# Two score banks for each exponential in an attention over 1920 keys

## The chip, the cores and the metric

The kernel runs on one core of one Trainium2 chip. The metric is the device time of one execution in microseconds (us); the median of several runs counts. Engines: PE is TensorE, ACT is ScalarE, DVE is VectorE, POOL is GpSimd, SP issues DMAs. PEld is PE's loading of weights, which runs beside its matmuls.

## The reference

A block of eight layers on x (16 batches, 256 tokens, 256 channels), each added to x. The change touches the fifth, an attention in which batches aren't kept apart: all 4096 tokens attend to the 16 x 120 = 1920 context tokens of all batches.

```python
# 8 heads, DIM_HEAD 128, SCALE = 128 ** -0.5
qh = _split_heads(jnp.einsum('bnq,qi->bni', x, Wq))
kh = _split_heads(jnp.einsum('bmc,ci->bmi', context, Wk))
vh = _split_heads(jnp.einsum('bmc,ci->bmi', context, Wv))
sim = jnp.einsum('hid,hjd->hij', qh, kh) * SCALE
mean = jnp.mean(sim, axis=-1, keepdims=True)
sim = (sim - mean) * ATTN_MATRIX_SCALE + mean
attn = jax.nn.softmax(sim, axis=-1)
out = jnp.einsum('hij,hjd->hid', attn, vh)
out = out.transpose(1, 2, 0, 3) ...
return jnp.einsum('bniv,iq->bnq', out, Wout) + bout
```

The mean falls out of the softmax, so the kernel takes exp(1.5 x SCALE x score - bias), with the row's maximum in the bias.

## The kernel before

The stage is `global_attention_stage`. The work goes by head (8), in a head by quad (8 quads of 512 tokens), in a quad by row tile j (4 of 128 tokens). The heads but the first and last run in a loop of the device. All products are exact to float32 by three passes of PE on a high and a low part of each operand (`three_passes`, L1811 to L1813): ACT writes the high part (`high`, L1739), DVE the rest (`low`, L1647).

While the probabilities of quad n are multiplied with the values, the scores and exponentials of quad n+1 are made, row tile by row tile. The orders are written by hand in a function `head` of each engine:

- PE, for row tile j: `scores` of j, one PSUM bank of 480 keys for each c (banks 0 to 3, 12 matmuls), then j's share of the 15 key tiles (4, 4, 4 and 3). A k-step waits for the low part of key tile k, turns key tile k+2 (`turn`, L1853: four transposes of a 128x128 block into bank 4 or 5) and makes the three passes on k. Between stand, for j=0, turns 0 and 1 and half of the output projection; for j=1 the other half (`output`, L1864); for j=2 `queries` of a later quad (L1834). `values` of a key share (L1828) stand in quad 0 of a head (before turn 8) and three times in the quad that turns the head.
- DVE: `maximum` (four maxima L1653, one over them, and the bias L1656), then `low_probs` of the key tiles turned in j.
- ACT: `high_probs` of the turned key tiles (two ahead for j=0, one for j=1 to 3) and between them the four exponentials of j, `exponential` (L1760), each out of one bank, with its sum in `part_sum`. In j=3 only key tile 14 is left to be turned, and the four follow one another.

The prob_t buffers are three deep, the banks for turns two. A bank of scores is free for PE when its exponential has raised `exped`. DVE's `sums` adds up `part_sum` once a quad. Before the first head, the first quad's scores, exponentials and values are made without other work beside them.

Of the kernel before, what the change touches and what calls it, by code (L numbers as in the profile page):

```python
# [22 lines left out]
ACT = mybir.ActivationFunctionType  # L23
AX = mybir.AxisListType

P = 128
# [1427 lines left out]
def global_attention_stage(nc, w, ctx):  # L1454
# [7 lines left out]
    chunk = 4 * NCTX  # L1462
    chunks = B // 4
    KEYS = B * NCTX
    KT = KEYS // P
    QT = 4
# [10 lines left out]
    def sb(name, shape, dt=F32):  # L1477
        return ctx.enter_context(nc.sbuf_tensor(f"global_{name}", shape, dt))
# [14 lines left out]
    q_high, q_low = sb("q_high", [P, 2, QW], F32R), sb("q_low", [P, 2, QW], F32R)  # L1493
    spare = w.held["spare"]
    prob = [spare[:, 0:QT * KEYS].rearrange("p (j c) -> p j c", j=QT), sb("prob", [P, QT, KEYS])]
    part_sum = sb("part_sum", [P, 2, QT, chunks])
    inverse = sb("inverse", [P, 2, QT])

    top = sb("top", [P, chunks])
# [13 lines left out]
    scores_psum, bias_ready, exped = sig("scores_psum"), sig("shifted"), sig("exped")  # L1513
# [18 lines left out]
    with nc.Block() as block:  # L1532
        @block.sync
        def _(sp):
            sp.dma_start(bout[:, :], io["L2_xattn_bout"].partition_broadcast(P)).then_inc(bout_loaded.sem, 16)
            sp.dma_start(ctx_t[:, :, :], io["ctx_t"].rearrange("(k p) b j -> p k (b j)", p=CP)
                         ).then_inc(loaded.sem, 16)
# [62 lines left out]
    def over_heads(eng, head):  # L1600

        head(0, True, False)
        with eng.Fori(1, heads - 1) as h:
            head(h, False, False)
        head(heads - 1, False, True)

    with nc.Block() as block:
# [126 lines left out]
        @block.scalar  # L1734
        def _(act):
            def high(dst, psum, is_there, n, ready):

                act.wait_ge(is_there.sem, is_there.count(n))
                act.activation(dst, psum, ACT.Copy).then_inc(ready.sem, 1)  # L1739

            def high_queries(n, par):
                high(q_high[:, par, :], w.psum[:, 7, :], q_psum, n, q_high_ready)

            def high_keys(h, c):
                high(k_high[:, c * chunk:(c + 1) * chunk], w.psum[:, c, 0:chunk], k_psum, h * chunks + c,
                     k_high_ready)

            def high_values(h, s, bank):
                tiles = slice(shares[s][0], shares[s][-1] + 1)
                high(v_high[:, tiles, :], w.psum[:, bank, 0:len(shares[s]) * dim]  # L1750
                     .rearrange("p (k d) -> p k d", d=dim), v_psum, h * QT + s, v_high_ready)

            def high_probs(n, k):
                high(prob_t_high[:, k % RING, :], w.psum[:, 4 + k % 2, :], prob_t_psum, n * KT + k, high_ready)

            def exponential(n, par, j, c):

                if c == 0:
                    act.wait_ge(bias_ready.sem, bias_ready.count(n * QT + j))
                act.activation(prob[par][:, j, c * chunk:(c + 1) * chunk], w.psum[:, c, 0:chunk], ACT.Exp,  # L1760
                               bias=bias[:, j % 2:j % 2 + 1], scale=scale,
                               accum_out=part_sum[:, par, j, c:c + 1]).then_inc(exped.sem, 1)

            def head(h, first, last):
                for t in range(QUADS):
                    n = h * QUADS + t
                    after = not (last and t == LAST)
                    turns_head = t == LAST and after
                    for j in range(QT):
                        ahead = list(turned_in[j])  # L1770
                        if j == 2 and not (last and t >= LAST - 1):
                            high_queries(n + 2, t % 2)
                        if turns_head and j == 0:
                            for c in range(chunks):
                                high_keys(h + 1, c)
                            lead = 5
                        else:
                            lead = 2 if j == 0 else 1
                        for k in ahead[:lead]:
                            high_probs(n, k)  # L1780
                        for c in range(chunks):
                            if after:
                                exponential(n + 1, (t + 1) % 2, j, c)
                            if t == 0 and j == 1 and c == 1:
                                high_values(h, 3, 7)
                            if turns_head and (j, c) in ((1, 1), (2, 1), (3, 0)):
                                high_values(h + 1, j - 1, 7)
                            for k in ahead[lead + c:lead + c + 1]:
                                high_probs(n, k)
                    act.wait_ge(attn_psum.sem, attn_psum.count(n))  # L1790
                    act.activation(attn_t[:, :], w.psum[:, 6, :], ACT.Copy).then_inc(attn_ready.sem, 1)

            for c in range(chunks):
                high_keys(0, c)
            high_queries(0, 0)
            for j in range(QT):
                for c in range(chunks):
                    exponential(0, 0, j, c)
                if j < 3:
                    high_values(0, j, 4 + j % 2)  # L1800
                if j == 2:
                    high_queries(1, 1)
            over_heads(act, head)

        @block.tensor
# [962 lines left out]
def chosen_attention_stage(nc, w, ctx):  # L2768
# [454 lines left out]
    ("last of all", experts_stage),  # L3223
    ("hold long", place_powers),
    ("compute", global_attention_stage),
    ("hold long", place_selective),
    ("compute", ternary_and_spectrum_stage),
# [88 lines left out]
```

## Time and profile before

| | |
|---|---|
| median of 3 runs | 4632.93 us (4632.79 to 4633.71) |
| the profiled execution | 4636.67 us |
| its span | 4634.9 us |
| PE busy | 4151.4 us |
| DVE busy | 3322.0 us |
| ACT busy | 2232.4 us |
| PE's mean granted clock | 0.946 |

The profile is of one execution. "Busy" counts the time in which at least one instruction of an engine runs; a matmul's duration includes its way through the array, so that PE's starts say more than its durations. "Idle before" is the time an engine stood still ahead of an instruction, and what released it. A granted clock of 1.00 is 2.4 GHz.

### The profile page before, as it was taken

What the parts mean: (1) busy time and instruction counts of PE and PEld (TensorE: products, weight loads), DVE (VectorE), ACT (ScalarE), POOL (GpSimd) and SP (SyncE); (2) the same over time, 40 slices, a digit from 0 to 9 for tenths busy, and PEclk for the clock granted to TensorE, in tenths of its full rate; (3) what the DMA queues carried; (4) which work ended last, traced back from release to release, by engine and by line L of the source; (5) the groups of instructions that cost most, each with busy time, mean ns of one, the idle gap of its engine ahead of it and who ended that gap; (6) DMA issues with size and microseconds to landing.
All of it is one profiled execution on the core that took longest, in us unless ns stands there. A gap on an engine that the chain in (4) does not pass through costs nothing. (4 is left out here: it accounts for less than half of the span.)

```text
span 4634.9 us, 72082 instructions
## 1 busy us (share of the span) xinstructions
PE 4151.4 (90%) x23376; PEld 3267.9 (71%) x23376; DVE 3322.0 (72%) x7934; ACT 2232.4 (48%) x5314; POOL 529.9 (11%) x982
## 2 busy tenths in 40 slices
PE   7998988999699999999999999999985888888686
PEld 6876766777387877778777777777863665656555
DVE  6985667666677777777777677777767888876455
ACT  3545655555365565655555555565531232322332
POOL 1331010111500000000000000001142111111300
PEclk9998999999799999999999999999975999989699
DMA  3000000000000000000000000000020000000101
GB/s 93 0 0 37 0 1 0 0 0 0 18 3 2 4 2 4 1 2 4 2 4 2 4 1 2 4 2 2 1 72 1 1 1 0 0 1 0 40 0 36
DMA packets 33797, 40.58 MB, mean 9 GB/s; under 512 B 5550, under 2 KB 30006, under 8 KB 33466
## 3 DMA queue, kind: packets, MB, share of 16 engines
q1 hardware_dynamic: 32732, 37.03, 2.7%
q8 instruction: 128, 2.10, 0.2%
q14 instruction: 137, 1.12, 0.1%
q10 hardware_dynamic: 800, 0.33, 0.0%
HBM read 32.90 MB, written 4.19 MB: 8 GB/s over the span
## 5 line engine op out<-in xcount | busy, mean ns | idle before, releaser
L1739 ACT ACTIVATE global_prob_t_high<-psum 128x512 fp32r<-128x512 f32 x960 | 570.7, 601 | 588.9 <-PE psum L1853 588.9
L1647 DVE TENSOR_TENSOR global_prob_t_low<-psum,global_prob_t_high 128x512 fp32r<-128x512 f32 x960 | 657.2, 690 | 251.0 <-ACT global_prob_t_high L1739 237.0
L1653 DVE TENSOR_REDUCE global_top<-psum 128x1 f32<-128x480 f32 x1024 | 666.9, 658 | 110.8 <-PE psum L1813 106.3
L1811 PE MATMUL psum<-global_prob_t_high,global_v_low 128*128 128x512 f32 x960 | 455.6, 475 | 1.0
L1811 PE MATMUL psum<-global_k_high,global_q_low 128*128 128x480 f32 x1024 | 390.6, 381 | 17.4 <-ACT spare L1760 14.8
L1813 PE MATMUL psum<-global_k_high,global_q_high 128*128 128x480 f32 x1024 | 391.1, 382 | 0.0
L1812 PE MATMUL psum<-global_k_low,global_q_high 128*128 128x480 f32 x1024 | 388.9, 380 | 0.0
L1812 PE MATMUL psum<-global_prob_t_low,global_v_high 128*128 128x512 f32 x960 | 379.7, 396 | 0.0
L1813 PE MATMUL psum<-global_prob_t_high,global_v_high 128*128 128x512 f32 x960 | 379.6, 395 | 0.0
L1760 ACT ACTIVATE spare<-psum,global_bias 128x480 f32<-128x480 f32 x512 | 337.8, 664 | 16.5 <-DVE global_bias L1656 15.1
L1760 ACT ACTIVATE global_prob<-psum,global_bias 128x480 f32<-128x480 f32 x512 | 337.9, 663 | 1.2
L1382 ACT ACTIVATE moe_gated<-psum,moe_weight 128x256 f32<-128x256 f32 x512 | 215.2, 472 | 228.3 <-PE psum L1436 212.9
L1853 PEld LDWEIGHTS psum<-ident,global_prob 128*128 128x128 f32 x1920 | 233.4, 141 | 99.3 <-DVE global_prob_t_low L1647 35.8
L1853 PEld LDWEIGHTS psum<-ident,spare 128*128 128x128 f32 x1920 | 234.0, 141 | 96.1 <-DVE global_prob_t_low L1647 33.6
L1853 PE MATMUL psum<-ident,global_prob 128*128 128x128 f32 x1920 | 284.1, 273 | 18.9 <-DVE global_prob_t_low L1647 17.9
L1853 PE MATMUL psum<-ident,spare 128*128 128x128 f32 x1920 | 284.2, 273 | 17.8 <-DVE global_prob_t_low L1647 17.8
L1811 PEld LDWEIGHTS psum<-global_k_high,global_q_low 128*128 128x128 f32 x1024 | 193.5, 189 | 59.9 <-ACT spare L1760 15.6
L390 POOL COPY powers<-ones 128x128 f32<-128x128 f32 x1 | 0.4, 414 | 1979.8 <-PE psum L1834 1979.8
L1812 PEld LDWEIGHTS psum<-global_k_low,global_q_high 128*128 128x128 f32 x1024 | 193.0, 189 | 33.5
L1813 PEld LDWEIGHTS psum<-global_k_high,global_q_high 128*128 128x128 f32 x1024 | 193.5, 189 | 29.7
L1813 PEld LDWEIGHTS psum<-global_prob_t_high,global_v_high 128*128 128x128 f32 x960 | 180.6, 188 | 42.3
L1434 PE MATMUL psum<-moe_we_high,moe_xn_low 128*128 128x512 f32 x512 | 204.1, 399 | 0.0
(455 smaller groups left out, 8593.3 us busy)
## 6 DMA issues: line engine op xcount, KB each, us to landing
x_res<-in_x SPq DMA_DIRECT2D x8, 512.0 KB, 9.8
moe_we<-in_expert_t SPq DMA_DIRECT2D x8, 512.0 KB, 7.6
out<-x_res SPq DMA_DIRECT2D x4, 1024.0 KB, 8.5
cho_wqkv<-in_L_ffn_Wqkv SPq DMA_DIRECT2D x2, 1536.0 KB
self_ctx_t<-in_ctx_t SPq DMA_DIRECT2D x2, 1440.0 KB, 13.6
sel_w<-in_L_xattn_W SPq DMA_DIRECT2D x2, 1024.0 KB, 11.2
global_ctx_t<-in_ctx_t SPq DMA_DIRECT2D x1, 1440.0 KB
sel_ctx_t<-in_ctx_t SPq DMA_DIRECT2D x1, 1440.0 KB
```

What stands on the lines that cost most here:

```text
L390: pool.tensor_copy(re[:, :, 0], w.ones[:, :])
L1382: last = act.activation(gated[:, local % RING, h, :], w.lane(s)[:, 1 + p % 3, h * D:(h + 1) * D], ACT.Relu, scale=weight[:, s, x:x + 1])
L1434: pe.matmul(bank, xn_low[:, s, k, :], we_high[pair], start=False, stop=False)
L1647: dve.tensor_tensor(dst, psum, high.bitcast(F32), ALU.subtract).then_inc(ready.sem, 1)
L1653: ins = dve.tensor_reduce(top[:, c:c + 1], w.psum[:, c, 0:chunk], AX.X, ALU.max)
L1739: act.activation(dst, psum, ACT.Copy).then_inc(ready.sem, 1)
L1760: act.activation(prob[par][:, j, c * chunk:(c + 1) * chunk], w.psum[:, c, 0:chunk], ACT.Exp, bias=bias[:, j % 2:j % 2 + 1], scale=scale, a ...
L1811: pe.matmul(to, lhs_low, rhs_high, start=start, stop=False)
L1812: pe.matmul(to, lhs_high, rhs_low, start=False, stop=False)
L1813: return pe.matmul(to, lhs_high, rhs_high, start=False, stop=stop)
L1853: last = pe.transpose(w.psum[:, 4 + k % 2, j * P:(j + 1) * P], prob[par][:, j, k * P:(k + 1) * P], w.ident[:, :])
```

## The change

An exponential reads two banks at once, 128 x 2 x 480 elements, and writes the 960 probabilities beside each other. `part_sum` holds two sums a row tile in place of four. The instruction raises `exped` by 2, so that all counts that other engines wait for stay as they were; a wait for bank 0 or 1 is now met when both have been read. The highs keep their places in the loop over c, where the calls for odd c fall out.

```diff
-    part_sum = sb("part_sum", [P, 2, QT, chunks])
+    part_sum = sb("part_sum", [P, 2, QT, chunks // 2])
...
-                act.activation(prob[par][:, j, c * chunk:(c + 1) * chunk], w.psum[:, c, 0:chunk], ACT.Exp,
+                act.activation(prob[par][:, j, c * chunk:(c + 2) * chunk].rearrange("p (c x) -> p c x", x=chunk),
+                               w.psum[:, c:c + 2, 0:chunk], ACT.Exp,
                                bias=bias[:, j % 2:j % 2 + 1], scale=scale,
-                               accum_out=part_sum[:, par, j, c:c + 1]).then_inc(exped.sem, 1)
+                               accum_out=part_sum[:, par, j, c // 2:c // 2 + 1]).then_inc(exped.sem, 2)
...
                         for c in range(chunks):
-                            if after:
+                            if after and c % 2 == 0:
                                 exponential(n + 1, (t + 1) % 2, j, c)
...
             for j in range(QT):
-                for c in range(chunks):
+                for c in range(0, chunks, 2):
                     exponential(0, 0, j, c)
```

ACT, a steady quad, row tile j=2 from the high part of the queries on, and j=3, before (`global_prob_t_high` is `high_probs`):

```order
L1739 ACTIVATE global_q_high<-psum 128x512
L1739 ACTIVATE global_prob_t_high<-psum 128x512
L1760 ACTIVATE spare,global_part_sum<-psum,global_bias 128x480
L1739 ACTIVATE global_prob_t_high<-psum 128x512
L1760 ACTIVATE spare,global_part_sum<-psum,global_bias 128x480
L1739 ACTIVATE global_prob_t_high<-psum 128x512
L1760 ACTIVATE spare,global_part_sum<-psum,global_bias 128x480
L1739 ACTIVATE global_prob_t_high<-psum 128x512
L1760 ACTIVATE spare,global_part_sum<-psum,global_bias 128x480
L1739 ACTIVATE global_prob_t_high<-psum 128x512
L1760 ACTIVATE spare,global_part_sum<-psum,global_bias 128x480 x4
L1791 ACTIVATE global_attn_t<-psum 128x512
```

The same place with the change:

```order
L1739 ACTIVATE global_q_high<-psum 128x512
L1739 ACTIVATE global_prob_t_high<-psum 128x512
L1760 ACTIVATE spare,global_part_sum<-psum,global_bias 128x960
L1739 ACTIVATE global_prob_t_high<-psum 128x512 x2
L1760 ACTIVATE spare,global_part_sum<-psum,global_bias 128x960
L1739 ACTIVATE global_prob_t_high<-psum 128x512 x2
L1760 ACTIVATE spare,global_part_sum<-psum,global_bias 128x960 x2
L1792 ACTIVATE global_attn_t<-psum 128x512
```

High 11 stands behind a pair now, high 12 right behind high 11, high 13 behind the second pair; the last high of the piece is high 14 of j=3. Row tile j=1 reads the same but for the queries. PE's and DVE's orders are unchanged.

## Rows read from the trace of the kernel before

**Rows 1.** Page, part 1: busy time of each engine, share of the span, instructions.

```profile
PE 4151.4 (90%) x23376; PEld 3267.9 (71%) x23376; DVE 3322.0 (72%) x7934; ACT 2232.4 (48%) x5314; POOL 529.9 (11%) x982
```

**Rows 2.** Busy time in the attention: us, PE, PEld, DVE, ACT, POOL, PEclk, DMA.

```profile
1278.00:3415.00 2137.00, 2089.55 (x11031) 1688.68 (x11029) 1583.39 (x2969) 1257.59 (x3159) 66.53 (x82) 1.00 0.01 3
```

**Rows 3.** Waits from 1278 to 3390 us: total, times, longest.

```profile
ACT global_prob_t_high L1739 <- PE psum L1853: 577.9, 259, 5.2
PE psum L1853 <- DVE global_prob_t_low L1647: 35.5, 63, 1.1
PE psum L1811 <- ACT spare L1760: 8.4, 5, 1.9
```

**Rows 4.** ScalarE's groups of instructions: count, busy us, mean ns, idle before.

```profile
L1739 ACT ACTIVATE global_prob_t_high<-psum 128x512 fp32r<-128x512 f32 x960 | 570.7, 601 | 588.9 <-PE psum L1853 588.9
L1760 ACT ACTIVATE spare<-psum,global_bias 128x480 f32<-128x480 f32 x512 | 337.8, 664 | 16.5 <-DVE global_bias L1656 15.1
L1043 ACT ACTIVATE self_prob<-psum 128x1920 f32<-128x1920 f32 x32 | 56.7, 1771 | 23.0 <-PE psum L1140 23.0
L680 ACT ACTIVATE self_prob<-self_prob 128x960 f32<-128x960 f32 x32 | 32.1, 1004 | 26.6 <-DVE self_prob L611 26.6
```

**Rows 5.** Timeline, row tile j=1: start us, us, engine, line, out<-in.

```profile
2133.83 0.66 ACT L1760 ACTIVATE spare<-psum,global_bias 128x480 f32<-128x480 f32 x1
2134.47 0.60 ACT L1739 ACTIVATE global_prob_t_high<-psum 128x512 fp32r<-128x512 f32 x1
2134.74 0.40 PE L1813 MATMUL psum<-global_prob_t_high,global_v_high 128*128 128x512 f32 x1
2134.97 0.66 ACT L1760 ACTIVATE spare<-psum,global_bias 128x480 f32<-128x480 f32 x1
2134.98 0.60 PE L1853 MATMUL psum<-ident,global_prob 128*128 128x128 f32 x4
2135.10 0.69 DVE L1647 TENSOR_TENSOR global_prob_t_low<-psum,global_prob_t_high 128x512 fp32r<-128x512 f32 x1 [0.44 <-ACT global_prob_t_high L1739]
2136.11 0.60 PE L1853 MATMUL psum<-ident,global_prob 128*128 128x128 f32 x4
```

**Rows 6.** Timeline of the same quad, row tile j=2 and the maxima of j=3.

```profile
2141.77 0.60 ACT L1739 ACTIVATE global_q_high<-psum 128x512 fp32r<-128x512 f32 x1 [3.79 <-PE psum L1834]
2142.74 0.67 ACT L1760 ACTIVATE spare<-psum,global_bias 128x480 f32<-128x480 f32 x1
2143.38 0.61 ACT L1739 ACTIVATE global_prob_t_high<-psum 128x512 fp32r<-128x512 f32 x1
2143.74 0.47 PEld L1853 LDWEIGHTS psum<-ident,global_prob 128*128 128x128 f32 x4 [0.17 <-DVE global_prob_t_low L1647]
2144.02 0.69 DVE L1647 TENSOR_TENSOR global_prob_t_low<-psum,global_prob_t_high 128x512 fp32r<-128x512 f32 x1 [0.33 <-ACT global_prob_t_high L1739]
2144.99 0.60 PE L1853 MATMUL psum<-ident,global_prob 128*128 128x128 f32 x4
2146.28 0.69 DVE L1647 TENSOR_TENSOR global_prob_t_low<-psum,global_prob_t_high 128x512 fp32r<-128x512 f32 x1 [0.44 <-ACT global_prob_t_high L1739]
2146.97 2.61 DVE L1653 TENSOR_REDUCE global_top<-psum 128x1 f32<-128x480 f32 x4
```

**Rows 7.** Timeline of the same quad, its last pass.

```profile
2149.99 0.69 DVE L1647 TENSOR_TENSOR global_prob_t_low<-psum,global_prob_t_high 128x512 fp32r<-128x512 f32 x1
2150.74 0.50 PE L1811 MATMUL psum<-global_prob_t_high,global_v_low 128*128 128x512 f32 x1
```

**Rows 8.** Timeline elsewhere: before the first head; a head's quad 0; low parts of j=0.

```profile
1255.15 0.61 ACT L1739 ACTIVATE global_v_high<-psum 128x512 fp32r<-128x512 f32 x1
...
1273.78 0.74 PE L1811 MATMUL psum<-global_k_high,global_q_low 128*128 128x480 f32 x1 [4.38 <-ACT spare L1760]
...
2101.63 1.50 PE L1828 MATMUL psum<-global_wv,global_ctx_t 96*128 96x128 f32 x12
...
2123.89 1.29 DVE L1647 TENSOR_TENSOR global_prob_t_low<-psum,global_prob_t_high 128x512 fp32r<-128x512 f32 x2
```

## The prediction

> **What bounds the kernel now.** I read the shares of busy time first, then the stretches of the attention over all contexts, then who waits for whom in it, and last the timeline of two row tiles. Of the whole span, PE is busy 90% and ScalarE 48% [rows 1]. The attention fills 1278 to 3415 us of it, 2137 us, and in it PE is busy for 2089.6 us (98%), at a granted clock of 1.00, its level of 2.4 GHz, while ScalarE is busy for 1257.6 us (59%) and VectorE for 1583.4 us (74%) [rows 2]. So PE sets the pace, and time is lost only where PE stands still. Of its waits, 35.5 us in 63 pieces stand before L1853 and end with a low part of VectorE: one of some 0.57 us at the start of each quad. Only 8.4 us in 5 pieces are put down to an exponential [rows 3]. ScalarE itself waits 577.9 us for PE's turns [rows 3]. By these sums ScalarE has room to spare. The timeline says something else: what room it has **where**.
>
> A row tile asks of ScalarE four exponentials and three or four `high_probs`, and these alternate. In row tile j=1 of a steady quad an exponential starts at 2133.83, high 7 at 2134.47, the next exponential at 2134.97 [rows 5]. That is 0.64 us for an exponential with the reading of its accumulator and 0.50 for a high, 1.14 us for the two. PE's k-step (a turn and three passes) lasts from 2134.98 to 2136.11 [rows 5]: 1.13 us. In these steps ScalarE is as full as PE. What it has too much of lies elsewhere, while PE computes scores.
>
> **How much room a high has.** The turn of key tile 9 waits for low 7, low 7 for high 7. Low 7 starts at 2135.10 and takes 0.69, so it ends at 2135.79; turn 9 starts at 2136.11 [rows 5]. In j=2 the weight load of turn 12 stood 0.17 us for low 10, until 2143.74, and turn 13 still came in time, at 2144.99 [rows 6]: a late load has a little room of its own. Where the wait is longer, at the last pass of a quad, low 14 ends at 2150.68 and load and matmul both start at 2150.74 [rows 7]; the first instruction then takes some 0.05 us more. So PE goes on about 0.1 us after the low part's end, and a high in j=1 may come about 0.2 us late before it costs anything.
>
> **The change, part by part.**
> *The instruction.* A copy of 512 elements takes 601 ns and the exponential of 1920 elements out of four banks 1771 ns [rows 4], 1170 ns for 1408 elements: 0.83 ns each, and no price for crossing banks in sight. So 480 more elements cost 0.40 us, and a pair takes 664 + 400 = 1064 ns [rows 4]. From the start of a pair to the next instruction: 0.64 + 0.40 = 1.04 us, where two took 1.28. ScalarE saves 512 x 0.24 = 123 us. None of it is on PE's path, since PE waits for an exponential nowhere in a steady quad: the scores of row tile j+1 come after the whole share of j.
>
> *What it moves.* The highs keep their order but stand differently: high, pair, high, high, pair, high in place of high, exp, high, exp, high, exp, high, exp. The high behind a pair starts 0.40 us later than it did behind one exponential; the high behind that has its turn to wait for and is on time.
>
> *j=1.* High 7 starts at 2133.83 + 1.04 = 2134.87 in place of 2134.47. Low 7 then ends at 2136.19, and turn 9 starts at about 2136.29 in place of 2136.11: **0.18 us** of new stall. High 9, behind the second pair, is 0.41 late, which delays the maxima of j=2; ScalarE waits 3.79 us for PE's queries at that point [rows 6], so this costs nothing.
>
> *j=2.* High 11 starts at 2142.74 + 1.04 = 2143.78 in place of 2143.38, low 11 at 2144.42 in place of 2144.02, ending at 2145.11; turn 13 starts at 2145.21 in place of 2144.99 [rows 6]: **0.22 us**. High 13 waits for the second pair and is 0.41 late, and low 13 starts at 2146.69 in place of 2146.28. VectorE's next instruction can start some 0.61 us after a low part (two of them take 1.29 us [rows 8], at 0.68 or 0.69 each), so the four maxima of j=3 start at 2147.30 in place of 2146.97 [rows 6], 0.33 late where PE is 0.22 late. The bias and low 14 hang on them, and PE already waits for low 14 [rows 7]: **0.11 us** more.
>
> *j=0 and j=3.* In j=0 the first pair starts while PE stands at the 0.57 us wait and is over before high 2 is due. High 4 is late, but its low part is needed only after the scores of j=1, which are twelve matmuls. In j=3 both pairs follow each other, with no high between them. Nothing, and nothing gained: the first scores of the next quad start later than the first pair ends.
>
> *The sum.* A quad has 0.18 + 0.22 + 0.11 = 0.51 us more. That holds for quads 1 to 6 of each of the 8 heads: 48 x 0.51 = 24.5 us. In quad 0 of a head the last value share lies between turns 7 and 9 (1.50 us of matmuls [rows 8]) and covers j=1: 8 x 0.33 = 2.6 us. In the 7 quads that turn the head such matmuls stand in j=1, 2 and 3; their scores of j=1 follow the exponentials closely, and I take 0.1 us each, an estimate: 0.7 us. Before the first head there is nothing to hide behind: in three of four row tiles VectorE's maxima wait for low values, these for the high values that start after four exponentials [rows 8], and come 0.48 us earlier (-1.4); for the fourth PE waits for the first exponential itself [rows 8], now 0.40 longer. Together -1.0. Sum: 24.5 + 2.6 + 0.7 - 1.0 = **+26.8 us**. The profiled execution took 4636.7 us (span 4634.9), 3.7 above the median; it would take 4663.5, and the median 4632.9 + 26.8 = **4660 us**.
>
> *Bounds of the unknown.* The pair's duration is in no row. Low end: an exponential of 960 elements in another stage took 1004 ns [rows 4], 60 ns under mine, which takes 0.06 from each of the two waits and leaves some 20 us. High end: a pair costs what two cost, 1.28 us; the highs are 0.64 late, 0.24 more at each of the two turns, 0.5 us a quad: 24 more, 4684. I take 1.04, as the row on four banks is nearest.
>
> **The rivals.**
> *A, faster: ScalarE paces the k-steps.* Its 1.14 and PE's 1.13 us are so close that PE might only follow. Then the 0.24 us that a pair saves is won for each pair of j=0 to 2: 2 x 3 x 48 x 0.24 = 69 us, 4564 us. It decides if PE could do a k-step faster than 1.13 us. Against it: a last pass at 2134.74 is followed by the turn at 2134.98 [rows 5], 0.24 us for a matmul that takes 0.40 to come through, with no row of idle time; and highs are released by turns, not by ScalarE (577.9 us of such waits [rows 3]). The Trainium skill speaks for the change here: ScalarE: Activation LUTs, in its rules for kernel authors, budgets about 0.3 us for every ACTIVATE beside 0.83 ns per element, so that fewer and longer ones should win. The trace agrees on the instruction (0.24 us saved) and says that the time saved is not PE's. Chance 6%.
> *B, no change: the lateness is absorbed.* If the turn buffers had 0.2 us more room than I read, all that is left is the start's gain, perhaps with some of the 8.4 us of rows 3: 4629 to 4637. Against it: the load of rows 6 that already waited 0.17 us. Chance 11%.
> *C, more than forecast: the pair is longer* (accumulating over two rows, or bank crossing), as the high end above, or a delay in j=1 carries on into later tiles: 4673 to 4690. Chance 13%.
> *D, the change doesn't do what it says*: both waits of a bank pair are on counts that the pair raises by 2, and the emitted program has half the exponentials, so I give it nothing.
>
> **The numbers.** The forecast (4644 to 4673 as its own range) has 70%. A change of under 0.2%, 9 us, cannot be told from none. Faster 0.06, from A; same 0.12, from B and a weak forecast; slower 0.82. The range leaves out A, most of B and the end of C: 4644 to 4684.
>
> **What would show it.** L1760 with 512 instructions of 128x960 at about 1064 ns, ScalarE some 120 us less busy; PE's own durations unchanged at clock 1.00; PE's waits at L1853 for low parts up from 35.5 us to about 55 (some 110 more pieces of about 0.2 us), in j=1 at turn 9 and in j=2 at turn 13; a steady quad 0.5 us longer. The forecast is wrong if highs behind a pair are late and PE's turns aren't, if PE's k-step falls under 1.13 us, or if the time comes from outside 1278 to 3450 us.

## The result and the profile after

The changed kernel takes 4650.45 us (median of 6 runs, 4646.94 to 4652.16) against 4633.32 us (6 runs, 4629.30 to 4637.71): +17.1 us, a ratio of 1.0036 with a 95% interval of 1.0026 to 1.0047. It is slower, by less than the 26.8 us of the forecast. The profiled execution took 4646.94 us with a span of 4645.2.

First the page, parts 1 and 5 of the changed kernel (they answer to [rows 1, 4]; lines behind L1760 have moved by one, so L1853 is now L1854):

```profile
PE 4162.5 (90%) x23376; PEld 3251.4 (70%) x23376; DVE 3295.9 (71%) x7934; ACT 2127.3 (46%) x4290; POOL 529.3 (11%) x982
...
L1739 ACT ACTIVATE global_prob_t_high<-psum 128x512 fp32r<-128x512 f32 x960 | 566.8, 597 | 677.2 <-PE psum L1854 664.0
...
L1760 ACT ACTIVATE spare<-psum,global_bias 128x960 f32<-128x960 f32 x256 | 271.0, 1060 | 19.4 <-DVE global_bias L1656 15.3
```

ScalarE has 1024 instructions fewer, 512 exponentials and 512 readings of the accumulator, and is 105 us less busy. The pair takes 1060 ns, against the 1064 of the forecast. PE counts as 11 us busier for the same 23376 matmuls. A matmul's time in the profile runs on for a while behind the start of the next one, so a stall of 0.1 to 0.2 us lies inside it and counts as busy; the rows of j=1 below show one.

The stretch of the attention (answers to [rows 2]), again at a granted clock of 1.00:

```profile
1278.00:3431.00 2153.00, 2108.02 (x11020) 1676.12 (x11020) 1555.41 (x2962) 1154.07 (x2149) 66.45 (x82) 1.00 0.01 3
```

2153 us for 2137, 16 us more, with ScalarE busy for 1154 us in place of 1258. Counted from the first matmul of the first queries to the start of the last four matmuls of the output projection, the two traces say it closer: 1245.3 to 3417.4 before, 1243.0 to 3433.1 after, 2172.1 and 2190.1 us. **+18.0 us are made there**, about as much as the medians differ by (17.1). The two profiled executions as a whole differ by less, 10.3 us (spans of 4634.9 and 4645.2): the changed one is 2.3 us shorter ahead of the attention and 5.4 us behind it, where the program is the same. Behind the attention the ten traces of this study last from 1212.1 us (the changed kernel's) to 1219.3, so I take this for scatter.

Who waits (answers to [rows 3]; total us, times, longest):

```profile
ACT global_prob_t_high L1739 <- PE psum L1854: 640.2, 359, 4.4
...
PEld psum L1854 <- DVE global_prob_t_low L1647: 111.8, 224, 1.2
...
PE psum L1854 <- DVE global_prob_t_low L1647: 35.2, 63, 1.2
...
PE psum L1812 <- ACT spare L1760: 3.7, 3, 1.3
```

and the one line of the kernel before that its rows didn't have:

```profile
PEld psum L1853 <- DVE global_prob_t_low L1647: 68.8, 123, 1.1
```

The waits of PE's matmuls before a turn have not changed (35.2 us for 35.5, still the one at each quad's start). Those of its weight loads have: 224 in place of 123, 101 more, 43 us more in total, a part of which a late load makes good. The new stalls stand in the loads' row alone, because the matmul before them still counts as busy.

Where they stand, the timeline of row tile j=1 of a steady quad shows (answers to [rows 5]):

```profile
2138.61 1.06 ACT L1760 ACTIVATE spare<-psum,global_bias 128x960 f32<-128x960 f32 x1
...
2139.64 0.59 ACT L1739 ACTIVATE global_prob_t_high<-psum 128x512 fp32r<-128x512 f32 x1
...
2140.27 1.45 DVE L1647 TENSOR_TENSOR global_prob_t_low<-psum,global_prob_t_high 128x512 fp32r<-128x512 f32 x2 [0.84 <-ACT global_prob_t_high L1739]
...
2140.66 0.39 PE L1814 MATMUL psum<-global_prob_t_high,global_v_high 128*128 128x512 f32 x1
...
2141.01 0.42 PEld L1854 LDWEIGHTS psum<-ident,global_prob 128*128 128x128 f32 x4 [0.39 <-DVE global_prob_t_low L1647]
2141.02 0.55 PE L1854 MATMUL psum<-ident,global_prob 128*128 128x128 f32 x3
```

The pair runs from 2138.61, high 7 starts at 2139.64, 1.03 us behind it. VectorE gets low 7 (the first of its two) at 2140.27. The load for turn 9 stands still for 0.39 us, and the turn starts at 2141.02 (its row ends where the window does, with three of its four matmuls), 0.36 us behind the last pass where 0.23 or 0.24 is usual. The last pass counts as busy for 0.39 us, until 2141.05, so PE shows no wait. Row tile j=2 (answers to [rows 6]) is the same with turn 13:

```profile
2147.72 1.06 ACT L1760 ACTIVATE spare<-psum,global_bias 128x960 f32<-128x960 f32 x1
...
2148.76 1.31 ACT L1739 ACTIVATE global_prob_t_high<-psum 128x512 fp32r<-128x512 f32 x2
...
2150.14 0.42 PEld L1854 LDWEIGHTS psum<-ident,global_prob 128*128 128x128 f32 x4 [0.44 <-DVE global_prob_t_low L1647]
```

I measure a quad from the first matmul of its queries to that of the next quad's. The 47 such intervals of quads 1 to 6 of a head (no values, no new keys in them) have a median of 32.00 us before and **32.38 us after**. In the six heads of the loop this length repeats to 0.06 us (it is 0.17 shorter in the first head and the last), where the whole time scatters by 8. It is the yardstick for the experiments.

Such an interval has 165 matmuls. Laid over each other from its first one on (medians of the 47), the starts before and after differ by 0.02 us at most up to turn 13; the turn's first matmul starts 0.17 us late, its second 0.23. From there to turn 9 the lateness stays between 0.20 and 0.25; behind turn 9 it is 0.39. Nothing lasting is added anywhere else, at the last pass of a quad either.

### The profile page after: what moved, and what is told of

Read it like the earlier page. It is cut to its first block and busy times, and to the rows that moved or that the text cites. A ratio compares the mean times of both kernels' runs of the same rounds, so it can differ in the third digit from the quotient of the medians.

```text
span 4645.2 us, 71314 instructions
## 1 busy us (share of the span) xinstructions
PE 4162.5 (90%) x23376; PEld 3251.4 (70%) x23376; DVE 3295.9 (71%) x7934; ACT 2127.3 (46%) x4290; POOL 529.3 (11%) x982
## 5 line engine op out<-in xcount | busy, mean ns | idle before, releaser
L1653 DVE TENSOR_REDUCE global_top<-psum 128x1 f32<-128x480 f32 x1024 | 652.6, 655 | 105.8 <-PE psum L1814 103.6
L1854 PEld LDWEIGHTS psum<-ident,spare 128*128 128x128 f32 x1920 | 228.9, 140 | 112.9 <-DVE global_prob_t_low L1647 57.5
L1854 PEld LDWEIGHTS psum<-ident,global_prob 128*128 128x128 f32 x1920 | 229.0, 140 | 112.5 <-DVE global_prob_t_low L1647 55.9
L1854 PE MATMUL psum<-ident,spare 128*128 128x128 f32 x1920 | 287.3, 275 | 18.7 <-DVE global_prob_t_low L1647 18.0
L1854 PE MATMUL psum<-ident,global_prob 128*128 128x128 f32 x1920 | 286.9, 274 | 18.7 <-DVE global_prob_t_low L1647 17.6
L1760 ACT ACTIVATE spare<-psum,global_bias 128x960 f32<-128x960 f32 x256 | 271.0, 1060 | 19.4 <-DVE global_bias L1656 15.3
L1760 ACT ACTIVATE global_prob<-psum,global_bias 128x960 f32<-128x960 f32 x256 | 270.8, 1059 | 3.4
```

What stands on the lines that cost most here:

```text
L1653: ins = dve.tensor_reduce(top[:, c:c + 1], w.psum[:, c, 0:chunk], AX.X, ALU.max)
L1760: act.activation(prob[par][:, j, c * chunk:(c + 2) * chunk].rearrange("p (c x) -> p c x", x=chunk), w.psum[:, c:c + 2, 0:chunk], ACT.Exp, ...
L1854: last = pe.transpose(w.psum[:, 4 + k % 2, j * P:(j + 1) * P], prob[par][:, j, k * P:(k + 1) * P], w.ident[:, :])
```

## The experiments

The theory: a high behind a pair starts 0.40 us late, VectorE's low part with it, and PE's turn of two key tiles further on has only 0.2 us of room; this happens once in j=1 and once in j=2. The rivals: the pair costs by itself, by its length or by what it reads; or PE is held because the first bank of a pair is handed over later.

**Pairs in some row tiles only.** One helper decides how many banks an exponential takes, `part_sum` keeps four slots (cleared once before the first head), and the rest is as in the change. Each kernel of this section ran 4 to 10 times:

```diff
+            def banks(j, c):
+                return (2, 0)[c % 2] if j in (0, 3) else 1     # second kernel: j == 1, third: j == 2
...
-                            if after:
+                            if after and banks(j, c):
                                 exponential(n + 1, (t + 1) % 2, j, c)
```

Pairs in j=0 and 3. 

> Pairs only in row tiles j=0 and j=3, single exponentials in j=1 and 2. Late highs (the theory): no high that PE waits for stands behind a pair, so a steady quad keeps the 32.00 us of before and the whole time stays within 3 us of before. Rival, a pair costs by itself, by the late release of its first bank or by its own length: about half of the 0.385 us a quad found with all pairs, 32.19 us a quad and some +9 us.

Pairs in j=1. 

> Pairs only in j=1. Late highs: high 7 is 0.4 us late, turn 9 stands 0.18 us more; a steady quad 32.18 us, none in quad 0 of a head (values cover it): about +9 us. If what the second pair does to the maxima of j=2 matters, more than 0.18.

Pairs in j=2. 

> Pairs only in j=2. Late highs: high 11 is late, turn 13 stands about 0.21 us more; a steady quad 32.21 us, +11 us. The prediction's further 0.11 us (maxima of j=3 late, low 14 late) would make it 32.32; the trace of the changed kernel says it is absorbed, as the last maximum waits for PE's last score.

The loads' waits before a turn in the three, in this order:

```profile
PEld psum L1860 <- DVE global_prob_t_low L1647: 68.0, 117, 1.1
```

```profile
PEld psum L1860 <- DVE global_prob_t_low L1647: 87.3, 164, 1.1
```

```profile
PEld psum L1860 <- DVE global_prob_t_low L1647: 92.5, 171, 1.2
```

| kernel | median us | ratio, 95% interval | steady quad | attention |
|---|---|---|---|---|
| before | 4632.35 (28 runs) | | 32.00 | 2172.1 |
| pairs in j=0 and 3 | 4636.28 (10 runs) | 1.0008 (0.9998 to 1.0017) | 31.97 | 2170.4 |
| pairs in j=1 | 4642.57 (10 runs) | 1.0022 (1.0013 to 1.0032) | 32.18 | 2179.9 |
| pairs in j=2 | 4644.58 (7 runs) | 1.0030 (1.0018 to 1.0041) | 32.23 | 2182.0 |

Half of the pairs, in j=0 and 3, cost a steady quad nothing and add no wait; those of j=1 add 41 waits and 0.18 us a quad; those of j=2 add 48 and 0.23. The two make 0.41, with the 0.03 that j=0 and 3 give back 0.38, as measured with all pairs: the parts add up. A pair doesn't cost by itself. The whole time with pairs in j=0 and 3 is 3.9 us above the kernel before, more than the 3 us I allowed, but its interval holds 1.0000: it can't be told from none, and the attention of its trace is 1.7 us shorter. The matmuls laid over each other say where the cost arises: with pairs in j=2 alone 0.23 us at turn 13 and nothing else, with pairs in j=1 alone 0.19 at turn 9 and nothing else.

**Which of the two pairs.** In all row tiles c=0 and c=1 are single and only the last two banks are a pair: `return (2, 0)[c % 2] if c >= 2 else 1`.

> In every row tile the first two exponentials are single, the last two a pair; so the highs of key tiles 7 and 11 come on time and only 4, 9 and 13 are late, whose turns no one waits for before the next scores. Late highs: a steady quad 32.00 us, time within 3 us of before, with 256 exponentials fewer. Rival, a pair costs by itself or any late high costs: half of 0.385 or more, 32.19 us.

Measured: 32.00 us a steady quad, attention 2173.0 us, 4636.38 us in all, ratio 1.0008 (0.9998 to 1.0017). The loads' waits before turns:

```profile
PEld psum L1860 <- DVE global_prob_t_low L1647: 67.8, 117, 1.1
```

So the second pair is free in a steady quad, also in j=1 and 2. It is the first pair's place, ahead of highs 7 and 11, that costs. The whole time is 4.0 us above the kernel before, where I had allowed 3. Most of it has a place: the interval that ends in j=2 of a quad that turns the head is 41.14 us long for 40.77 before, 7 x 0.37 = 2.6 us. There PE's scores of j=1 follow the exponentials of j=0 closely, and they wait for the second pair.

**A late handing over, without pairs.** The kernel before, with

```diff
-                        pe.wait_ge(exped.sem, exped.count((n * QT + j - 1) * chunks + c))
+                        pe.wait_ge(exped.sem, exped.count((n * QT + j - 1) * chunks + (c | 1)))
```

> Four single exponentials as before, but PE's scores of bank c wait for the exponential of bank c or 1, so banks 0 and 1 and banks 2 and 3 are handed over together, as a pair does it. Late highs: a steady quad stays at 32.00 us, since the scores come after the whole share. Only in the quad that turns the head, where the scores of j=1 follow the exponentials of j=0 closely, is a later release felt: up to the 0.2 us by which that quad grew with pairs in j=0. Time within 3 us of before. Rival, the cost of a pair is the late release of its first bank: 32.2 to 32.4 us a steady quad.

Measured: 31.99 us a steady quad; 4639.13 us against 4631.74 of the kernel before (15 runs beside this and the following kernels), +7.4 us, ratio 1.0013 (1.0004 to 1.0023). That is more than the 3 us expected. The time that I can place is in the quads that turn a head: the interval that ends in their j=2 is 41.43 us for 40.77 before, 7 x 0.66 = 4.6 us, which lies within the interval's 2 to 11 us. I had expected at most 0.2: in this kernel bank 0 waits until the second exponential is done, which stands behind a high, and that is later than the end of a pair. With pairs in j=0 and 3 alone the same interval is 40.96, 0.19 more than before. The waits for an exponential say the same, this kernel first, then the kernel before:

```profile
PEld psum L1853 <- DVE global_prob_t_low L1647: 68.7, 123, 1.1
...
PEld psum L1811 <- ACT spare L1760: 22.0, 31, 2.2
```

```profile
PEld psum L1811 <- ACT spare L1760: 14.3, 12, 2.3
```

So the rival has a small true core, at 7 places in the program, and none in the steady quads.

**The same lateness from another cause.** Four single exponentials, and in j=1 and 2 behind the first one

```diff
+                            if after and j in (1, 2) and c == 0:
+                                act.activation(prob[(t + 1) % 2][:, j, 3 * chunk:3 * chunk + PAD],
+                                               w.psum[:, 3, 0:PAD], ACT.Copy)     # PAD = 416
```

> Four single exponentials, with a copy of 416 elements behind the first one in j=1 and in j=2, about 0.40 us of ScalarE (its result is overwritten by the fourth exponential). Late highs: the same lateness of highs 7 and 11 from another cause must cost the same, 32.36 to 32.40 us a steady quad and 16 to 20 us in all, although ScalarE now works more than before, where with pairs it worked less. Rival, the cost belongs to the pair: 32.00 us.

Measured: 32.46 us a steady quad, attention 2195.7 us, 4656.37 us in all, +24.6 us, ratio 1.0048 (1.0033 to 1.0063): more than the 16 to 20 I expected. The timeline of its row tile j=1:

```profile
2142.64 0.65 ACT L1763 ACTIVATE spare<-psum,global_bias 128x480 f32<-128x480 f32 x1
...
2143.27 0.52 ACT L1788 ACTIVATE spare<-psum 128x416 f32<-128x416 f32 x1
...
2143.67 0.61 ACT L1742 ACTIVATE global_prob_t_high<-psum 128x512 fp32r<-128x512 f32 x1
...
2145.05 0.42 PEld L1859 LDWEIGHTS psum<-ident,global_prob 128*128 128x128 f32 x4 [0.41 <-DVE global_prob_t_low L1650]
```

High 7 starts 1.03 us behind the first exponential, as it does behind a pair, and the load waits for 0.41 us, as there (0.39). The matmuls laid over each other lose 0.23 us at turn 13 and 0.19 at turn 9, the same two places as with pairs (0.23 and 0.17). 0.46 us a quad is 0.08 more than with pairs. Of this 0.05 gather in small steps between the two turns (the lateness grows from 0.23 to 0.28), where with pairs 0.01 is given back; what makes the steps is not shown. The places are what the runs settle: ScalarE with *more* work and ScalarE with *less* work lose time at the same two turns, if the one high ahead of each is equally late.

**A version that uses the wait that is left.** The profile before shows what still stops PE: 0.57 us at the first turn of a quad, for low 0, which waits on VectorE behind `sums` (L1677, L1678; low 0 is the first of the two at 2123.89 [rows 8]). Nobody needs the sums before the next quad.

```profile
2123.37 0.17 DVE L1677 TENSOR_REDUCE global_inverse<-global_part_sum 128x4 f32<-128x16 f32 x1
2123.57 0.18 DVE L1678 RECIPROCAL global_inverse<-global_inverse 128x4 f32<-128x4 f32 x1
...
2124.64 0.66 PE L1853 MATMUL psum<-ident,global_prob 128*128 128x128 f32 x4 [0.57 <-DVE global_prob_t_low L1647]
```

```diff
-                        if j == 0:
-                            sums(n, t)
                         if j == 1 and before:
                             output(n - 1, (t - 1) % QUADS, 1)
+                        if j == 2:
+                            sums(n, t)
                         if j == 2 and not (last and t >= LAST - 1):
                             low_queries(n + 2, t % 2)
```

> The kernel before, with VectorE's sum of the partial sums and its reciprocal (0.45 us between them and low 0) moved from j=0 to j=2, ahead of the low part of the queries, where VectorE waits 1.3 us. Low 0 comes 0.45 us earlier, PE's wait of 0.57 us at the first turn of a quad shrinks to about 0.15: steady quad 31.58 us, 63 x 0.42 = 26 us less in all, 4606 us. If VectorE's output tile then blocks low 2, or low 0 waits for high 0 instead, the gain is smaller: 10 to 20 us.

Measured: 4606.07 us (4603.25 to 4609.56), ratio **0.9944 (0.9930 to 0.9957)**, 25.7 us faster than before; a steady quad 31.54 us, attention 2144.8 us. PE's waits for low parts, loads and matmuls:

```profile
PEld psum L1853 <- DVE global_prob_t_low L1647: 42.9, 118, 0.6
...
PE psum L1853 <- DVE global_prob_t_low L1647: 1.8, 9, 0.2
```

The matmuls' 35.5 us are 1.8 now. In j=2 the sums and the reciprocal run in the hole that VectorE had there, between the bias and the low part of the queries:

```profile
2125.97 0.15 DVE L1656 TENSOR_SCALAR global_bias<-global_bias 128x1 f32<-128x1 f32 x1
2126.09 0.17 DVE L1677 TENSOR_REDUCE global_inverse<-global_part_sum 128x4 f32<-128x16 f32 x1
...
2126.29 0.18 DVE L1678 RECIPROCAL global_inverse<-global_inverse 128x4 f32<-128x4 f32 x1
...
2127.43 0.69 DVE L1647 TENSOR_TENSOR global_q_low<-psum,global_q_high 128x512 fp32r<-128x512 f32 x1 [0.96 <-ACT global_q_high L1739]
```

With the last two exponentials of each row tile as a pair on top of it:

> The same, with the last two exponentials of every row tile as a pair. With highs 7 and 11 on time it must be equal to the kernel with late sums and single exponentials within 3 us (a steady quad equal within 0.05 us): what ScalarE saves is nobody's bound. If ScalarE did pace a part of the quad, it would be faster, by up to 0.24 us a quad.

Measured: 4608.88 us, ratio 0.9950 (0.9935 to 0.9965), steady quad 31.54 us, attention 2145.2 us. The steady quad is equal to that of the version without pairs. The whole is 2.8 us longer, within the 3 expected; the intervals that end in a quad that turns a head are 0.38 us longer, much as above, which makes 2.7. With 256 exponentials fewer and PE's wait at the first turn gone, ScalarE's time is still not what paces a steady quad.

## Why the prediction was right, and where its size was off

*What bounds the kernel.* Right: PE paces the attention, and ScalarE's sum of busy time said nothing about the change. 105 us less of it came with 18 us more of time.

*The pair.* Forecast 1064 ns and 1.04 us to the next instruction; measured 1060 ns and 1.03 us. No cost of crossing a bank shows. Both bounds around it were far off.

*ScalarE's busy time.* Forecast some 120 us less, measured 105. The 0.24 us for each exponential was right; not in the sum is that ScalarE's work now falls into more pieces. Between 1245 and 3420 us it has 676 stretches of unbroken work where it had 472, and at the end of each no next instruction overlaps the last one (0.60 us for a high in place of 0.50). 204 x 0.10 = 20 us is an estimate from these figures.

*j=1.* Forecast 0.18 us at turn 9; measured 0.17 there, and 0.18 a quad with pairs in j=1 alone. The high behind the second pair costs nothing, as said. In quad 0 of a head the values cover it: from a new head's first score to the queries of its quad 0 PE takes 21.5 us, before and after.

*j=2, turn 13.* Forecast 0.22; measured 0.23 there, with all pairs and with pairs in j=2 alone.

*j=2, the maxima of j=3.* **This step failed**: "the four maxima of j=3 start at 2147.30 in place of 2146.97, 0.33 late where PE is 0.22 late. The bias and low 14 hang on them": 0.11 us more. The timeline after:

```profile
2151.63 0.69 DVE L1647 TENSOR_TENSOR global_prob_t_low<-psum,global_prob_t_high 128x512 fp32r<-128x512 f32 x1 [0.84 <-ACT global_prob_t_high L1739]
...
2152.24 2.56 DVE L1653 TENSOR_REDUCE global_top<-psum 128x1 f32<-128x480 f32 x4
...
2153.72 0.38 PE L1814 MATMUL psum<-global_k_high,global_q_high 128*128 128x480 f32 x1
...
2155.20 0.69 DVE L1647 TENSOR_TENSOR global_prob_t_low<-psum,global_prob_t_high 128x512 fp32r<-128x512 f32 x1
...
2155.95 0.19 PEld L1812 LDWEIGHTS psum<-global_prob_t_high,global_v_low 128*128 128x128 f32 x1 [0.45 <-DVE global_prob_t_low L1647]
```

The row of the kernel before that belongs beside it, with the maxima of [rows 6]:

```profile
2148.51 0.38 PE L1813 MATMUL psum<-global_k_high,global_q_high 128*128 128x480 f32 x1
```

The maxima do start late, 0.09 us behind the first score's end. But four of them take 2.56 us now in place of 2.61, and the bias hangs on the *last* one, which can't start before PE's last score is through: that ends at 2148.89 before (2148.51 + 0.38) and the maxima at 2149.58, 0.69 later; after, 2154.10 and 2154.80, 0.70 later. The chain goes by PE, not by VectorE's start, and the load of the last pass waits 0.45 us, as it did (0.46). The starts of PE's matmuls say the same: nothing is added at the last pass, with all pairs or with pairs in j=2 alone. In 56 quads this is 0.11 x 56 = 6.2 us of the 8.8 us by which the attention's +18.0 is short of the sum's 26.8.

*The quads that turn a head.* Forecast 0.1 us each, estimated. In the interval that ends in their j=2 the growth is 0.43 us; 0.23 of it is turn 13 of the quad ahead, so 0.2 us each are left, as with pairs in j=0 and 3 (0.19): under-sized by 0.7 us in all.

*Before the first head.* Forecast -1.0 us; the first two intervals give 0.05 - 0.92 = -0.9. The parts are right too: from one row tile's maxima to the next 6.57 us became 6.15 (7.16 became 6.73 for the last), three times some 0.43 less where 0.48 was forecast, and from the last maxima to PE's scores 3.65 became 4.10, 0.45 more where 0.40 was. PE's wait there, 3.92 us where [rows 8] has 4.38, is shorter only because the maxima came earlier.

*The rest.* The intervals add up: the 47 of quads 1 to 6 grew by 18.3 us together, the 7 that end in a quad that turns a head by 3.0, the stretch behind the last queries by 0.3; the first two shrank by 0.9, and the 7 across a head's end by 2.8. That is the +18.0. The forecast had nothing for the 2.8. One of the 7 intervals makes 1.65 of them, with a drop of the clock in the trace before (below) that other kernels of this study have in another head or not at all. The others go with PE's stops between heads (below): 8.4 us in all before, 6.9 after. These stops vary without pairs as well as with them (6.4 us with pairs in j=2 alone, 8.4 with the last two exponentials as a pair), so I count the 2.8 as no effect of the change; that is argued, not shown. Without them the change costs 20.8 us, and nearly all of what is missing from 26.8 is the step that failed.

*The signs.* PE's waits for low parts at L1853 were to rise from 35.5 to about 55 us, some 110 more pieces. They stayed at 35.2: the stalls came, but as 101 more pieces, 43 us, in the row of the loads. A steady quad is 0.38 us longer, not 0.5.

*The rivals.* A, ScalarE as the pace, is refuted twice: PE's k-step is not shorter with 0.24 us less of ScalarE in it, and with PE's wait at the first turn gone pairs still gain a steady quad nothing. B would have needed 0.2 us more of room. C, a longer pair, did not occur, nor did a delay grow in later tiles. The Trainium skill's page ScalarE: Activation LUTs, in its rules for kernel authors, budgets about 0.3 us for every ACTIVATE. The trace agrees nearly, with 2 x 0.64 - 1.03 = 0.25 us saved for each one less; but this is ScalarE's time, and the time here is PE's.

## What to carry to other kernels

Merging two instructions takes away fixed cost on the engine, and puts everything that stood between them later by the length of the second. Where short work that another engine waits for is interleaved with long work, look for the latest start that each short piece can bear, and merge only where none stands behind: the same merge was free in six of the eight places of a steady quad here. An engine whose busy share is 59% can be full just where it matters, and a busy share falls by a merge without the time falling. And where an engine waits, look ahead of the work it waits for in that queue: moving 0.45 us of sums that nobody needed yet gave 25.7 us, where no version of the merge gave any.

## What the runs showed of the hardware

An exponential with a bias per partition and an accumulated sum, out of two banks of 480 elements, takes 1060 ns; out of one bank 664 [rows 4]. That is 396 ns for 480 elements, 0.83 ns each, as between the copy of 512 elements and the exponential of 1920 in the prediction. So no cost of the bank's edge shows, with the accumulated sum either.

PE's clock can fall for a few microseconds within a stage that shows 1.00. PE stands still for 1.2 to 1.9 us, before and after, between heads at the five places where the loop of the device jumps back, and not at its entry or exit. The profile names an exponential for most of these stops, but in the trace before the one whose bank PE wants next starts at 2895.22 and takes 0.66 us, so it ended 4.5 us before PE goes on at 2900.34. It isn't the cause; what is, is open. Behind the longest stop of the trace before, 1.91 us, the matmuls of the new head take 0.60 us and start 0.40 apart, from 2900.66 to 2903.46, and then 0.38 again:

```profile
2900.34 0.53 PE L1811 MATMUL psum<-global_k_high,global_q_low 128*128 128x480 f32 x1 [1.91 <-ACT spare L1760]
...
2900.66 0.60 PE L1812 MATMUL psum<-global_k_low,global_q_high 128*128 128x480 f32 x1
...
2903.46 0.60 PE L1813 MATMUL psum<-global_k_high,global_q_high 128*128 128x480 f32 x1
...
2904.17 0.38 PE L1812 MATMUL psum<-global_k_low,global_q_high 128*128 128x480 f32 x1
```

The stretch in which they lie has a granted clock of 0.50, the level of 1.2 GHz:

```profile
2902.00:2904.00 2.00, 2.00 (x7) 1.65 (x6) 1.01 (x2) 0.00 (x0) 0.00 (x0) 0.50 0.00 0
```

Behind another head, after 1.87 us, nothing of it is seen:

```profile
2628.73 0.48 PE L1811 MATMUL psum<-global_k_high,global_q_low 128*128 128x480 f32 x1 [1.87 <-ACT spare L1760]
2629.05 0.38 PE L1812 MATMUL psum<-global_k_low,global_q_high 128*128 128x480 f32 x1
```

The interval across the slowed head's end is 40.38 us long, for 38.3 to 38.8 at the four heads before it. One such outlier, some 1.7 us longer than its neighbours, is also in the traces of pairs in j=1, of the late handing over, of the padded kernel and of late sums with single exponentials, each time with a granted clock of 0.50 for some microseconds behind the stop; it is in none of the other five. The stops ahead of it lasted 1.87, 1.81, 1.75 and 1.77 us. Yet stops of 1.87 us (this one, and one with the last two exponentials as a pair) and of 1.82 (the changed kernel) were followed by a clock of 1.00, so a stop's length alone doesn't decide it. It is a reason to compare a stage by its repeated part.
